# Shared up blocks ahead of the last tokens, down weights in quarters, and a router that makes its masks first

## The reference

```python
x = x + attention(layernorm(x), wq, wk, wv, wo)   # causal, 32 query heads, 8 key/value heads, head size 16
flat = layernorm(x)                               # 2048 x 512
logits = flat @ router_w                          # 64 experts
idx = top_k(logits + router_bias, 4)
gate = softmax(logits) at idx, divided by its sum over the four
routed = sum over the 4 experts e of gate_e * ((silu(flat @ wg[e]) * (flat @ wu[e])) @ wd[e])   # F = 128
shared = sum over 2 experts s of (silu(flat @ swg[s]) * (flat @ swu[s])) @ swd[s]               # 512 hidden each
x = x + routed + shared
```

## Time and profile before

| | |
|---|---|
| runs | 1267.17, 1269.21, 1269.75 us; median 1269.21 |
| profiled execution | 1262.9 us, of which the profiled span is 1261.1 us |
| granted TensorE clock, mean | 0.98 |
| second stage ends (last logits) | 588.86 us from the span's start |
| first routed instruction on TensorE | 738.48 us from the span's start |

### The profile page before, as it was taken

The page is one execution under the profiler, slowest core; times in us unless marked ns, Lnnn a source line. Parts: engine busy times, 40 slices in busy tenths (PEclk is TensorE's granted clock), DMA queues, the critical chain, the costliest instruction groups (busy, mean ns, idle before and its releaser), DMA issues.

```text
span 1261.1 us, 27442 instructions
## 1 busy us (share of the span) xinstructions
PE 1140.0 (90%) x8998; PEld 519.1 (41%) x8998; DVE 750.5 (60%) x1223; ACT 496.2 (39%) x936; POOL 367.5 (29%) x470
## 2 busy tenths in 40 slices
PE   5976899889889888999789989999999989999898
PEld 3523233333333332455334445545454544544343
DVE  6656899999999993667977212333232222327373
ACT  3212778878878879134310112222222212212010
POOL 5000222222222222104736112332332322227461
PEclk9987999999999999999899999999999999999899
DMA  8344212322311300322000347878887789747552
GB/s 234 112 115 108 40 40 57 59 38 45 69 38 38 75 20 2 134 103 98 0 1 1 118 178 250 271 255 267 296 287 219 226 293 314 258 109 233 159 167 67
DMA packets 75765, 169.97 MB, mean 135 GB/s; under 512 B 13764, under 2 KB 16324, under 8 KB 75716
## 3 DMA queue, kind: packets, MB, share of 16 engines
q1 hardware_dynamic: 45972, 100.59, 26.7%
q0 software_dynamic: 12800, 41.95, 11.7%
q10 hardware_dynamic: 16944, 26.75, 6.2%
HBM read 225.08 MB, written 41.42 MB: 211 GB/s over the span
## 4 chain that ended last, share of the span: by engine, by line
PE 57%; DVE 20%; issue 8%; DMA 7%; POOL 3%; ACT 3%; SPq 1%; DVEq 0%; ACTq 0%; POOLq 0%
PE PS L1217 13%; PE PS L1233 7%; DVE maxes L1289 7%; PE PS L1169 6%; PE PS L1043 5%; PE PS L1190 5%; PE PS L1095 4%; DVE max_low L1291 4%; PE PS L1204 4%; PE PS L931 4%; DMA ring<-in_L_ffn_wg_dram 3%; PE PS L992 2%; POOL ring L769 2%; PE PS L1021 2%; PE PS L1225 2%
## 5 line engine op out<-in xcount | busy, mean ns | idle before, releaser
L825 ACT ACTIVATE att<-PS 128x512 f32<-128x512 f32 x576 | 312.5, 594 | 90.4 <-PE PS L1021 84.9
L1289 DVE TENSOR_REDUCE maxes<-PS 128x2 f32<-128x128 f32 (+7 forms) x256 | 186.4, 747 | 31.1 <-PE PS L936 30.9
L1169 PE MATMUL PS<-XN,att 128*128 128x512 f16 x768 | 171.6, 386 | 13.6 <-POOL w_att L733 8.0
L1043 PE MATMUL PS<-att,v_head 128*32 128x256 f32 (+1 forms) x2560 | 178.6, 370 | 0.9 <-POOL att L662 0.9
L931 PE MATMUL PS<-att 48*128 48x512 f16 (+7 forms) x768 | 127.6, 330 | 52.6 <-DVE max_low L1291 24.2
L1291 DVE TENSOR_REDUCE max_low<-PS 128x2 f32<-128x1024 f32 x128 | 154.7, 1208 | 11.2 <-PE PS L931 11.0
L1590 DVE COPY w_att<-PS 128x512 f32<-128x512 f32 x96 | 66.4, 691 | 108.2 <-DMA slot_y<-w_att 81.1
L883 ACT ACTIVATE w_att<-PS 128x512 f32<-128x512 f32 x96 | 57.2, 597 | 172.6 <-PE PS L1204 172.6
L1578 DVE TENSOR_TENSOR w_att<-w_att,PS 128x128 f32<-128x128 f32 x96 | 27.5, 287 | 161.8 <-ACT w_att L888 161.6
L662 POOL TENSOR_SCALAR_AFFINE_SELECT att<-att 128x512 f32<-128x512 f32 (+1 forms) x96 | 75.1, 789 | 162.4 <-ACT att L825 161.2
L1169 PEld LDWEIGHTS PS<-XN,att 128*128 128x128 f16 x768 | 75.7, 99 | 107.9 <-POOL w_att L733 8.5
(11 more groups left out here) (170 smaller groups left out, 1334.4 us busy)
## 6 DMA issues: line engine op xcount, KB each, us to landing
ring<-in_L_ffn_wg_dram SPq DMA_DIRECT2D x96, 512.0 KB
XT<-in_L_ffn_wg_dram SPq DMA_DIRECT2D x96, 512.0 KB
ring<-in_L_ffn_wd_dram SPq DMA_DIRECT2D x96, 256.0 KB
XT<-in_L_ffn_wd_dram SPq DMA_DIRECT2D x96, 256.0 KB
slot_y<-w_att ACTq DMA_DIRECT2D x192, 128.0 KB
att<-q_stacks SPq DMA_DIRECT2D x64, 192.0 KB, 3.9
q_stacks<-att SPq DMA_DIRECT2D x24, 256.0 KB
att<-k_stacks SPq DMA_DIRECT2D x64, 96.0 KB, 4.1
```

The lines of the kernel that those rows point to most:

```text
L825: act.activation(probs[:, n0 % RING, u * BANK:(u + 1) * BANK], bank((2 * n0 + u) % EXP_BANKS), ACT.Exp, scale=HD ** -0.5 / QK_SCALE ** 2). ...
L1043: mm = pe.matmul(PS[32 * r:32 * r + 32, at:at + qn], v_head[b][:, kt, :], probs[:, (NS * b + s) % RING, a:a + qn], start=s in (0, NS0), st ...
L1169: mm = pe.matmul(bank(2 * (n % 2) + k), shared_w[:, 2 * k + w, C * s + c, at:at + P], v[:, c, tokens], start=(c == 0 and w == 0 and v is x ...
L1289: dve.reduce_max(maxes[b][:, :, t], src, AXX).then_inc(side_read, 1)
```

## The change

Five things are done:

1. **Two up blocks ahead.** TensorE does blocks 0 and 1 right after the last projections, ahead of the turning and the logits of token tiles 8 to 15.
2. **Down weights in quarters.** Scaling, high part and low part are each done in four pieces, most of them between the shared products.
3. **GpSimd also makes the products and low parts of blocks 8 to 11** (`ON_POOL` = 12); ScalarE copies those up banks too. The token rows go between and behind them.
4. **Masks first, gates last.** VectorE makes only the one-hots and the mask before `masks_ready`; the four gate products and sums are spread later. ScalarE's exponential comes after SiLU of block 1. `shared_add` of the first four tiles is spread through the slot and gate work. `cum` is gone.
5. **TensorE sums over the tiles.** In its place `ranks` adds, for each tile, `ones_b` times its mask to all later tiles, and counts with 16 one-column matmuls. `table` moves from after block 12 to after block 14.

```diff
-TABLE_AT = HC + 4
+AHEAD_UP = 2
+TABLE_AT = HC + 6
+ON_POOL = HC + 4
...
 # GpSimd
-            for k in range(2):
-                pool.wait_ge(stage_in[k], 16 * 3)
-                pool.tensor_scalar(w_stage[:, k, :], w_stage[:, k, :], W_SCALE, None, ALU.mult).then_inc(swd_scaled, 1)
-            for k in range(2):
-                pool.wait_ge(swd_hi_ready, k + 1)
...
+            swd_scale(0)
+            swd_scale(1)
+            for n in range(ON_POOL):
+                if n == HC:
+                    hidden_low(n - 1)
+
+                    pool.wait_ge(down_done, 4)
                 pool.wait_ge(silu_done, n + 1)
                 pool.wait_ge(up_copied, n + 1)
                 if n >= 2:
                     pool.wait_ge(hidden_lo_done, n - 1)
                 pool.tensor_tensor(hidden(n), silu_s[:, n % 2, :], up_s[:, n % 2, :], ALU.mult)\
                     .then_inc(hidden_done, 1)
-                if n:
+                if n and n != HC:
                     hidden_low(n - 1)
+                if n in (1, 2):
+                    swd_scale(n + 1)
+                if n in (3, 4, 5, 6):
+                    swd_low(n - 3)
+                if n in (ON_POOL - 2, ON_POOL - 1):
+                    token_row(n - (ON_POOL - 2))
+            hidden_low(ON_POOL - 1)
+            for k in range(2, TOPK):
+                token_row(k)
 # ScalarE
-            for k in range(2):
-                act.wait_ge(swd_scaled, k + 1)
...
-                    if g == 0:
+                    if n < ON_POOL:
                         act.activation(up_s[:, n % 2, :], bank(2 * (n % 2) + 1), ACT.Copy,
                                        scale=1 / W_SCALE).then_inc(up_copied, 1)
+                    if n == AHEAD_UP - 1:
+                        act.wait_ge(route, 2)
+                        act.activation(ex[:, :, :], tmp[:, :, :], ACT.Exp).then_inc(ex_ready, 1)
                     if n > HC * g:
                         hidden_high(n - 1)
+                    for half in {2: (0, 1), 4: (2,), 5: (3,)}.get(n, ()):
+                        swd_high(half)
 # TensorE
+                if g == 4:
+                    pe.wait_ge(x1_done, NT)
+                    pe.wait_ge(w_lo_ready, 3)
+                    pe.wait_ge(x_lo_ready, 4)
+                    for hc in range(AHEAD_UP):
+                        shared_up(0, hc)
...
-                    pe.matmul(bank(6 + h), ones_b[:, :], flat(cum), start=False, stop=True)
+                    for t in range(end - 1):
+                        after = max(t + 1, first)
+                        at = (6 + h) * BANK + (after - first) * E
+                        pe.matmul(PS[:, at:(7 + h) * BANK].rearrange("p (t e) -> p t e", e=E), ones_b[:, :],
+                                  mask[:, t, :].unsqueeze(1).to_broadcast([P, end - after, E]),
+                                  start=False, stop=t == end - 2)
+                for t in range(NT):
+                    mm = pe.matmul(bank(4, 1)[0:E, :], mask[:, t, :], ones_b[:, 0:1], start=t == 0, stop=t == NT - 1)
 # VectorE
-            dve.wait_ge(ex_ready, 1)
             for k in range(TOPK):
                 step(dve.tensor_tensor(onehot[k][:, :, :], iota_e[:, :].unsqueeze(1).to_broadcast(all_te),
                                        idxf[:, :, k:k + 1].to_broadcast(all_te), ALU.is_equal))
-                step(dve.tensor_tensor(tmp[:, :, :], onehot[k][:, :, :], ex[:, :, :], ALU.mult))
-                step(dve.tensor_reduce(part_k[:, k, :], tmp[:, :, :], AXX, ALU.add))
...
-            for t in range(1, NT):
-                step(dve.tensor_tensor(cum[:, t, :], cum[:, t - 1, :], mask[:, t - 1, :], ALU.add))
...
+            dve.wait_ge(ex_ready, 1)
+            gate_part(0)
             dve.wait_ge(starts_done, 1)
...
             for k in range(TOPK):
-                step(dve.tensor_tensor(tmp[:, :, :], onehot[k][:, :, :], pos[:, :, :], ALU.mult))
-                step(dve.tensor_reduce(part_k[:, k, :], tmp[:, :, :], AXX, ALU.add))
+                slot_part(k)
+                if k == 2:
+                    shared_add(0)
...
+            for t in range(1, TOPK):
+                shared_add(t)
+                gate_part(t)
```

## The result

The changed kernel takes 1258.49 us (median of 8 runs, 1252.08 to 1266.88) beside 1266.54 for the kernel before (8 runs, 1262.53 to 1269.75). The ratio over all runs is 0.9946 (the two medians alone give 0.9936), with an interval from 0.9924 to 0.9968: faster by 0.5%, some 6.8 us, with 4.1 to 9.6 us possible. The prediction was 1262.7 against 1269.2, a ratio of 0.9949.

The account below looks back on a forecast made before the run. TensorE was taken as the bound, with waits for GpSimd and VectorE; 738.5 - 731.9 = 6.6 us, less 0.1 clock, gave 1256.4 us profiled, times 1.005, 1262.7 us; range 1256.0 to 1268.5 (70%).

Parts of the forecast that it names:

- The sum: Instruction lists carried forward: first routed instruction at 731.9 instead of 738.5 us, 6.6 us gained, less 0.1 for clock.
- Blocks 0 and 1: After attention: start at 575.7, routing at 600.3, block 2 at 601.2 after a 1.4 us wait, 6.0 us ahead.
- Quarters: Down-weight pieces between GpSimd's products: late once, 1.5 us before block 5, which ends at 623.5 instead of 629.5.
- Masks: VectorE's one-hots and sums: 7.1 us free, 16.3 with hold-ups; masks at 625.9 instead of 633.2, TensorE waits 2.4.
- Ranks: TensorE's sums over the tiles: 4.5 us (4.1 to 7.1) in place of 1.4, ending at 630.4; lead shrinks to 4.2.
- Expert list: Before the down matmuls: held up twice, comes at 641.8, 0.9 us of wait; spread additions cost nothing.
- Blocks 8 to 15: No wait before block 10, at 673.2 instead of 683.72; waits of 1.1 before block 12, 3.0 before 13.
- The clock rival: TensorE's clock drops after narrow work and short waits; blocks 2 and 3 low would be 3.9 us slower, 1273.1; 8%.
- my own sign of being wrong: The prediction counted as wrong if the clock fell below 0.9 in 600 to 640 us; a second sign concerned late products.
- GpSimd as the bound: GpSimd's products, low parts, quarters and token rows, held by VectorE, eat the gain: 1269.4, no change; 12%.
- the larger gain: Quarters and token rows fit between one-hots, so waits shrink: 14.5 us gained if all gone, 1254.7; 10%.
- My rule: GpSimd operations and VectorE ones with two SBUF inputs exclude each other; without it the working would end at 723, not 731.9.

Follow-up runs that it names:

- e6: Changed kernel, all down-weight scalings, low and high parts ahead of products and first SiLU; stage (token tile 8's first turning matmul to first routed instruction) 161.93 us.
- e1: Changed kernel with blocks 0 and 1 again behind the last logits; stage 153.55 us against 157.64.
- e10: Changed kernel with ScalarE's table load, SiLU and up copy of block 0 ahead of its copies of token tiles 12 to 15; stage 157.00 us against 157.64.
- e12: The kernel of e1, timed against the kernel before the change: 1258.19 us, ratio 0.9953 (0.9933 to 0.9973).
- e8: e1 with two pairs of one-hot rows before the gates and the running sum on VectorE; stage 144.37 us; timed, 1247.76 us, ratio 0.9864 to the kernel before.
- e9: Changed kernel with the running sum of the masks on VectorE again and TensorE's ranks of five matmuls; stage 166.33 us against 157.64.

## Why the prediction was right, step by step

The sum was right, 6.6 us of the stage against 6.04, but partly because errors cancelled. Taking 2.06 us off the changed kernel's times puts both profiles on one clock. On it the ranks end at 627.0, 3.4 us ahead of the working's 630.4; block 10 starts at 671.5, only 1.7 ahead of 673.2; and the routed experts start at 732.4, 0.5 behind 731.9. The rest of the forecast was part luck too: the profiled execution was to take 1256.4 us and took 1264.95, since 2 us more came ahead of the stage and 6 behind it, while "as long as before" was predicted; and the base of 1269.21 us was the median of three runs, where eight give 1266.54. Less 6.5 that would have been 1260.0; the median was 1258.49.

- **Blocks 0 and 1.** Wrong place: not at 575.7, but at 581.6, between the turning of tiles 8 to 11 and that of 12 to 15. Routing started at 599.1, predicted 600.3, and the wait before block 2 was 1.62, predicted 1.4. The step credits this part and the quarters together with 6.0 us at block 2 (601.2 predicted, 600.6 measured). That lead is the quarters' (e6 brings the 8.44 us wait back with the blocks ahead in place); the blocks ahead cost 4.1 of the stage (e1).
- **Quarters.** The predicted wait of 1.5 us before block 5 did not come. The clock, of which this step had nothing, took 1.3 instead: block 5 ended at 622.8, predicted 623.5.
- **Masks.** Predicted 9.2 us of hold-ups, measured 4.4 (11.5 us from the first one-hot to the last mask sum, 7.1 free). The masks came at 620.0, not 625.9, and the wait of 2.4 us did not come.
- **Ranks.** Predicted 4.5 us within 4.1 to 7.1. From the first row that the changed kernel's trace shows it is 629.09 - 624.93 = 4.16, but the first `tri` matmul is missing there; e10 and e12, which show it, give 4.4. 16 one-column matmuls took 0.67.
- **Expert list.** Wait 0.9 predicted, 1.51 measured; part of it is a small operation held up, shown below. An addition costs 0.87 where I had nothing: "the spread additions cost nothing" was wrong, and the kernel before had 0.94 for the same addition.
- **Blocks 8 to 15.** Waits of 1.1 and 3.0 predicted, 1.08 and 2.94 measured. The clock's 1.7 us at block 13 was missing: the sum had 0.1 for clock.
- **Rivals.** The clock rival was half right: losses of 1.3 and 1.7 us, far from the 6.5 that would decide. But my own sign of being wrong, a clock below 0.9 in 600 to 640, did come in its first slice, 0.83, as above (0.96 over the four together): it was no sign of the outcome, since a slice of 0.83 cost only 1.3 us. GpSimd as the bound did not come; the larger gain is there, but in another order (e8), not in this one.

## What to carry to other kernels

Before work is moved ahead to fill a wait, ask what hangs on the work that it displaces: here two blocks put ahead of the last logits cost 4.1 us of the stage, 2.9 through ScalarE's list and 1.2 through VectorE's, though the timed runs do not show them in the whole time. The same instruction list can be a gain or a loss by its place: the running sum cost 8.7 us where the masks had 2.8 us to spare and saved 2.95 where they were early, so after each reordering ask again which engine is late next. Where two engines shut each other out, put the long instruction of the one where the other is idle.

## What the runs showed of the hardware beyond the prediction

- **The exclusion takes in operations with one SBUF input too.** In the changed kernel (GpSimd, then VectorE), a scaling of 24x8 numbers took 2.05 us, until GpSimd's low part was over; before, with no GpSimd operation beside it, it took 0.16. My rule named only operations with two SBUF inputs, though the copy of 128x128 from which I read it has one.

```profile
638.94 2.12 POOL L729 TENSOR_TENSOR att<-ring,att 128x1024 f16<-128x1024 f32 x1
639.03 2.05 DVE L1554 TENSOR_SCALAR small<-small 24x8 f32<-24x8 f32 x1
```

- **The same wait costs different clock.** After a wait of 2.93 or 2.94 us before block 13, the next 48 matmuls took 12.22 us in the changed kernel, e1, e9 and e12, 10.53 in e6 and 13.45 in e10. After 3.04 us the kernel before lost nothing. What decides is not in these rows.
- **A broadcast operand runs at nearly full rate.** The ranks' matmuls, 17 x 512 columns with one tile's mask read for up to eight tiles, took 3.79 us in e10 (625.12 to 628.91): 0.22 us for 512 columns, as in the blocks (24 matmuls of 512 in 5.2 us).
- **No drain beside the table load.** The load begins 0.01 us after the copy before it and SiLU 0.01 us after the load. The 1.38 us that the Trainium skill adds (ScalarE: Activation LUTs, "What ACT_TABLE_LOAD costs") do not show.
